# A decoder layer: first stage and self attention in one program, over shared buffers and PSUM banks, with unit 0's row maxima behind the last value copy

## What is computed

```python
q = proj(WQ_w, WQ_b)
k = proj(WK_w, WK_b)
v = proj(WV_w, WV_b)
q = _apply_rope(q, cos, sin)
k = _apply_rope(k, cos, sin)
scores = jnp.einsum('bhqd,bhkd->bhqk', q, k) / jnp.sqrt(jnp.asarray(D_K, x.dtype))
scores = jnp.where(causal[None, None, :, :], scores, -jnp.inf)
attn = jax.nn.softmax(scores, axis=-1)
out = jnp.einsum('bhqk,bhkd->bhqd', attn, v)
```

## Time and profile before

| | us |
|---|---|
| median of 3 runs | 1196.13 |
| all runs | 1196.43, 1190.45, 1196.13 |
| the profiled execution, its own time | 1199.54 |
| its span, first to last instruction | 1197.8 |
| busy in the span: PE / DVE / ACT / POOL | 1032.9 / 865.8 / 591.1 / 288.3 |
| mean granted TensorE clock (1.00 is 2.4 GHz, 0.50 is 1.2 GHz) | 0.918 |

### The profile page before, as it was taken

The page is one execution under the profiler, slowest core; times in us unless marked ns, Lnnn a source line. Parts: engine busy times, 40 slices in busy tenths (PEclk is TensorE's granted clock), DMA queues, the critical chain, the costliest instruction groups (busy, mean ns, idle before and its releaser), DMA issues. The chain is left out here.

```text
span 1197.8 us, 17928 instructions
## 1 busy us (share of the span) xinstructions
PE 1032.9 (86%) x6184; PEld 509.8 (43%) x6184; DVE 865.8 (72%) x1770; ACT 591.1 (49%) x819; POOL 288.3 (24%) x268
## 2 busy tenths in 40 slices
PE   7629999989999999989889779989889769889960
PEld 4312333333333333326778622322323218678850
DVE  5839999878898888604789968887778815645545
ACT  1311466656766667774644226645555443333322
POOL 6720101220510300012310055402020211322225
PEclk9956999999999999999999959998989888999995
DMA  5450279190200000000101034201010001242225
GB/s 192 156 145 1 36 72 106 22 154 25 56 1 1 2 1 2 1 1 31 53 27 38 1 107 144 65 25 57 23 63 28 27 26 44 68 141 73 71 83 168
DMA packets 60825, 70.04 MB, mean 58 GB/s; under 512 B 10364, under 2 KB 53756, under 8 KB 60732
## 3 DMA queue, kind: packets, MB, share of 16 engines
q1 hardware_dynamic: 55212, 57.40, 20.5%
q0 software_dynamic: 3408, 9.34, 2.2%
q10 hardware_dynamic: 2112, 2.10, 0.5%
HBM read 45.37 MB, written 22.85 MB: 57 GB/s over the span
## 5 line engine op out<-in xcount | busy, mean ns | idle before, releaser
L573 DVE TENSOR_REDUCE self_piece_max<-self_max 128x1 f32<-128x512 f32 (+3 forms) x640 | 349.6, 603 | 49.5 <-PE self_max L475 29.3
L540 ACT ACTIVATE self_probs<-self_scores 128x1024 f32<-128x1024 f32 (+3 forms) x320 | 274.3, 896 | 196.5 <-PE self_scores L494 195.5
L475 PE MATMUL self_max<-stack_k,stack_q 96*128 96x512 bf16 (+3 forms) x640 | 209.8, 366 | 6.0 <-DVE self_piece_max L573 3.9
L1732 DVE TENSOR_REDUCE cross_piece_max<-banks 128x1 f32<-128x512 f32 x256 | 164.3, 683 | 40.7 <-PE banks L1622 39.0
L1704 ACT ACTIVATE cross_probs<-banks 128x1024 f32<-128x1024 f32 x128 | 126.7, 1023 | 108.3 <-PE banks L1645 102.4
L494 PE MATMUL self_scores<-stack_q,stack_k 98*128 98x512 bf16 (+3 forms) x640 | 171.1, 351 | 7.2 <-DMA stack_q<-self_shift 5.9
L505 PE MATMUL self_out<-self_probs,V 128*17 128x512 f32 (+3 forms) x1280 | 148.4, 536 | 2.6 <-ACT self_probs L540 2.0
L475 PEld LDWEIGHTS self_max<-stack_k,stack_q 96*128 96x128 bf16 x640 | 62.3, 98 | 172.8 <-DVE self_piece_max L573 129.3
L451 POOL TENSOR_SCALAR_AFFINE_SELECT self_probs<-self_probs 128x512 f32<-128x512 f32 x64 | 40.8, 637 | 382.2 <-ACT self_probs L540 381.9
L1622 PE MATMUL banks<-kx_few,stackx 97*128 97x512 bf16 x256 | 99.9, 432 | 18.8 <-DVE cross_shift L1743 6.9
L1645 PE MATMUL banks<-stackx,kx_few 99*128 99x512 bf16 x256 | 83.0, 410 | 0.7 <-DMA stackx<-cross_shift 0.6
(11 more groups left out here) (315 smaller groups left out, 1554.9 us busy)
## 6 DMA issues: line engine op xcount, KB each, us to landing
stack_q<-qparts SPq DMA_DIRECT2D x96, 64.0 KB, 6.7
stackx<-xparts SPq DMA_DIRECT2D x96, 64.0 KB, 2.3
xin<-sent SPq DMA_DIRECT2D x39, 129.0 KB
stack_k<-kparts SPq DMA_DIRECT2D x18, 256.0 KB, 11.3
qparts<-parts SPq DMA_DIRECT2D x8, 384.0 KB, 2.6
kparts<-parts SPq DMA_DIRECT2D x8, 384.0 KB, 3.0
xparts<-xparts_sb SPq DMA_DIRECT2D x8, 384.0 KB, 2.7
o_tok<-in_w SPq DMA_DIRECT2D x4, 768.0 KB, 5.4
```

The source lines that it names most:

```text
L475: mm = nc.tensor.matmul(slot[:, 0:pc["w"]], pc["lhsT"], pc["rhs"], start=True, stop=not pc["diag"])
L540: nc.scalar.activation(probs[:, i % 3, 2 * pair:2 * pair + 2, st["off"]:C], ps[:, 2 * pair:2 * pair + 2, st["off"]:C], ACT.Exp, scale=SCAL ...
L573: nc.vector.tensor_reduce(piece_max[:, u % 2, pc["row"], pc["at"]:pc["at"] + 1], slot[:, 0:pc["w"]], AX.X, ALU.max).then_inc(side_read, 1)
L1732: nc.vector.tensor_reduce(piece_max[:, u % 2, pc["row"], pc["at"]:pc["at"] + 1], slot[:, 0:pc["w"]], AX.X, ALU.max).then_inc(side_read, 1)
```

## The change

The two blocks become one, so the barrier between them goes, and SP's waits for all stores and for chunks 0 to 2 with it. For that the two stages must live in memory together. Two large buffers, `early` and `late`, are cut into views of both stages: `probs` lies over the inputs of the projections, the later stacks over cosines, `rest`, `turned`, `crossed` and `whole`. PSUM is one tile of 8 banks: the projection products take banks 0 to 3 (later the scores), the values 4 and 5 (later `po` and one piece bank), and the pieces 6, 7 and 5. The values thus have two banks instead of four, and PE waits for the value copy of unit n - 2 instead of n - 4.

Unit 0's pieces and turn stand behind the last projection product on PE, and on DVE between the remainders of pair 6 and those of pair 7. SP sends shift 0 ahead of the stores of units 14 and 15, and loads chunk 2 of group 0 behind it instead of among the stores; chunk 3 is loaded behind shift 1. ACT waits for chunk 0's and 2's stores before it writes `acc_sb`, which now lies over `parts`.

```diff
+            early = sb(att, "early", [P, 3 * GH * C])
+            late = sb(att, "late", [P, 36 * C + 44])
...
+            xT_sb = early_part(0, KD * T).rearrange("p (k t) -> p k t", k=KD)
+            w_sb = early_part(KD * T, 3 * KD * D).rearrange("p (w k d) -> p w k d", w=3, k=KD)
+            bv_all = early_part(KD * T + 3 * KD * D, D)
+            probs = early[:].rearrange("p (n j c) -> p n j c", n=3, j=GH)
...
+            cs = late_part(0, 2 * T).rearrange("p (n t) -> p n t", n=2)
+            rest = late_part(8, 4 * C).rearrange("p (n c) -> p n c", n=4)
+            turned = late_part(12, 4 * C).rearrange("p (n h c) -> p n h c", n=2, h=2)
+            crossed = late_part(16, 4 * C).rearrange("p (n h c) -> p n h c", n=2, h=2)
+            whole = late_part(20, 4 * C).rearrange("p (n c) -> p n c", n=4)
+            parts = late_part(24, 12 * C).bitcast(BF16).rearrange("p (n r c) -> p n r c", n=SLOTS, r=3)
+            acc_sb = late_part(24, 2 * C).rearrange("p (n c) -> p n c", n=2)
+            raw = late_part(26, 2 * (MP2 // 3)).rearrange("p (n c) -> p n c", n=2)
+            last_q = late[:, 28 * C + 44:36 * C + 44].bitcast(BF16)
...
+            stack_q += [rows.rearrange("p (c h t) -> p c h t", c=NC, h=GH) for rows in (halves(16), last_q)] + stack_q
...
+            stack_k += [rows.rearrange("p (h t) -> p h t", h=GH) for rows in (halves(0), halves(8))] + stack_k
...
+            banks = psum(att, "self_banks", [P, 8, C])
+            pq = banks[:, 0:4].rearrange("p (n h) c -> p n h c", n=2)
+            pv = banks[:, 4:6]
+            ps, po = banks[:, 0:4], banks[:, 4]
+
+            def pm(n):
+                return banks[:, (6, 7, 5)[n % SB]]
...
-                pq = psum(stage, "pq", [P, 2, KD, C])
-                pv = psum(stage, "pv", [P, 4, C])
...
-                        for i in range(2):
-                            sp.wait_ge(s_parts_out[i], 8 * len(units))
-                        sp.wait_ge(consts_in, 32)
-                        for c in range(NC - 1):
-                            sp.wait_ge(s_load[c], 16 * 2 * len(PAIRS))
...
+                    def send_shift(u):
+                        sp.wait_ge(shift_ready, u + 1)
+                        for b, dst in enumerate(works[u]["shift_to"]):
+                            sp.dma_start(dst, shift[:, u % 2, b]).then_inc(shift_in[u % 2], 16)
...
+                    for n, (t, m, c) in enumerate(units):
+                        dst = (qparts, kparts)[t].rearrange("r (p m) t -> m p r t", m=KD)[m, :, :, c * C:(c + 1) * C]
+                        if n == len(units) - KD:
+                            send_shift(0)
+                            sp.wait_ge(s_parts_out[(NC - 2) % 2], 16 * TC * (NC // 2))
+                            load(NC - 2)
+                        sp.wait_ge(p3_ready, n + 1)
+                        sp.dma_start(dst, parts[:, n % SLOTS]).then_inc(s_parts_out[c % 2], 16)
+                        if 0 < c < NC - 1 and n % 4:
+                            if n % 4 == 1:
+                                sp.wait_ge(s_parts_out[(c - 1) % 2], 16 * TC * ((c + 1) // 2))
+                            for to, there in loads[c - 1][(n % 4 - 1) * 4:n % 4 * 4]:
+                                sp.dma_start(to, there).then_inc(s_load[c - 1], 16)
+
+                    for u in range(1, len(works)):
+                        send_shift(u)
+                        if u == 1:
                             for i in range(2):
...
+                                sp.wait_ge(s_parts_out[i], 8 * len(units))
+                            load(NC - 1)
+                        if u in (2, 3):
+                            load(u + 2)
...
+                    pool.wait_ge(p3_ready, len(units))
...
+                        if n >= 2:
+                            pe.wait_ge(v_read, n - 1)
+                        for k in range(KD):
+                            last = nc.tensor.matmul(pv[:, n % 2, 0:D], xT_sb[:, k, n * P:(n + 1) * P], w_sb[:, 2, k, :],
+                                                    start=(k == 0), stop=(k == KD - 1))
...
+                        if n == 2:
+                            pe.wait_ge(v_read, len(units))
+                        if n >= SB:
...
+                    pe.wait_ge(s_ones, 7)
+                    for item in before:
+                        side_item(item)
+                    for n in range(C // P):
+                        nc.tensor.matmul(po[:, n * P:(n + 1) * P], zeros[:], zeros[:], start=True, stop=True)
...
+                        if u == 0:
+                            act.wait_ge(s_parts_out[0], 8 * len(units))
...
+                    def remainders(pair):
+                        for n in (KD * pair, KD * pair + 1):
+                            dve.wait_ge(p1_ready, n + 1)
+                            if n >= 4:
+                                dve.wait_ge(p3_ready, n - 3)
+                            nc.vector.tensor_tensor(rest[:, n % 4], whole[:, n % 4], parts[:, n % SLOTS, 0], ALU.subtract).then_inc(rest_ready, 1)
...
+                        if pair:
+                            remainders(pair - 1)
...
+                    for item in before:
+                        side_item(item)
+                    remainders(len(units) // KD - 1)
+                    for third in thirds:
+                        for item in third[0] + third[1] + third[2]:
+                            side_item(item)
```

More of the change, by code:

```diff
@@ new lines, in decoder_layer @@
+            ones_rows = [stack_k[g][KS:KS + 2, :, c * C:(c + 1) * C] for g in range(NG - 1) for c in range(NC)]
+            steps, works, first_of, before, thirds, diag_before = schedule(steps, works)
+            extra_parts = [(kt_view(there), to[0][:], to[1][:]) for there, to in ((xwq, xwq_sb), (xwkv, wkv_sb))]
+            for k in range(KD):
+                for a in range(0, MP2, MP2 // 3):
+                    extra_parts.append((ctxT[k * P:(k + 1) * P, a:a + MP2 // 3].rearrange("(o p) d -> p o d", o=1),
+                                        ctx2[0][:, k:k + 1, a:a + MP2 // 3], ctx2[1][:, k:k + 1, a:a + MP2 // 3]))
```

721 lines of the change are left out of this document (318 added, 403 removed).

## The result

The changed kernel takes 1177.1 us (median of 4 runs, 1174.5 to 1180.42), the kernel before 1194.76 beside it (median of 4, 1190.45 to 1196.43). The ratio is 0.9858, with a 95% interval of 0.9833 to 0.9882: faster by 17.7 us. Forecast were 1175.8 us and 20.35 us off, and a range of 1168 to 1182. The total held. One term of the sum did not, and most of what follows is about it.

A forecast was written before the change was run, and what follows sets the result against it. The seam before self attention was taken as one serial chain ending at step 0's scores (89.50). Starting them at 69.0, less 0.15, saves 20.35 us: 1196.13 becomes 1175.8 us, range 1168 to 1182.

The forecast's parts named there:

- (1): Unit 0's reductions on DVE: start at 57.52, shift 0 ready 8.30 us later, at 65.82.
- (5): Two V banks instead of four in the projection stage: 0.15 us lost; 6 us if the cover failed in all seven pairs.
- (2): SP's queue: shift 0, behind the stores of units 12 and 13, is issued at 66.0.
- (3): Shift 0's transfer: landed and scores of step 0 started at 69.0, between bounds of 68.4 and 69.6.
- (4): Zeroing matmuls on PE, 2.05 us, between the transpose and step 0: hidden in the wait for the shift, cost nothing.
- (6): Remainders of pair 7 on DVE move from 61.56 to about 65.9, hidden in DVE's wait for step 0.
- (7): SP's queue behind shift 0: chunk 2's 12 loads take 5.5 us, landed by 76, 11 us to spare; later stores delayed harmlessly.
- A: Rival: TensorE's full clock returns earlier after the seam, 1.2 us more gain, at most 2.6 (1173 to 1174.6); chance 0.12.
- B: Rival: late transfers or V banks cause new waits, 1182 to 1189 us; chance 0.11 together with milder forms of D.
- C: Rival: half clock lasts into steps behind the seam where PE is the bound, slower than before, some 1202 us; chance 0.04.
- D: Rival: PE's pieces or shift 0 still wait for the whole first stage, 1187 us; milder forms share 0.11 with B.

The follow-up runs named there:

- four_banks: The changed kernel with four V banks instead of two, PE's first piece of unit 0 waiting for the last value copy; ratio to the kernel before 0.9833.
- merge_only: The changed kernel with both SP's order and DVE's order undone, leaving one block without a barrier and two V banks; ratio to the kernel before 0.9883.
- sp_order_before: The changed kernel with only SP's order undone: shift 0 and chunk 2's loads back behind all stores or among them; 1184.85 us, ratio 0.9922.
- after_again: The changed kernel itself, unchanged, run and profiled once more; 1177.3 us, ratio to the kernel before 0.9864.
- values_behind_pair: The changed kernel, two V banks, PE issuing both value products behind the pair's second projection product; ratio 0.9792, run again 0.9825 (1171.63 us).
- rest_behind_sums: The changed kernel with DVE waiting, ahead of a pair's remainders, until POOL's sums of the next pair are done; ratio to the kernel before 0.9878.
- before_second: The kernel before, unchanged (four V banks), profiled a second time; 1196.01 us.
- pieces_ahead: values_behind_pair with PE issuing 12 pieces of unit 1 ahead of step 0's scores instead of behind them; 1168.26 us, ratio to the kernel before 0.9782.

## Why the prediction was right, and where it was not

**(1) Shift ready 8.30 us behind the first reduction.** Right: 64.55 to 72.46 + 0.28 = 72.74, 8.19 us. The starting point, 57.52, was wrong, by (5).

**(2) and (3) Issue and landing.** In the changed kernel the stores of units 12 and 13 are long out when the shift is ready, so (2) doesn't bind, and the scores start 75.18 - 72.77 = 2.41 us behind the issue, which is the idle-queue row again. In four_banks, where the shift stands right behind these stores, the issue comes 53.63 us from t1 (forecast 66.0 - 12.90 = 53.10), and the scores 2.55 us later (forecast 3.0). The two errors of half a microsecond cancel: 56.18 against 69.0 - 12.90 = 56.10. The ordered-write rule of the Trainium skill ("DMA: Bandwidth & Descriptors", queues, rings and completion order) is not contradicted: in four_banks the store of unit 13, issued at 66.4, landed in 2.6 us, at 69.0, and the first shift row behind it took 2.3 us instead of 1.7, to 69.2. It costs little here: issued 0.5 us behind the store, the first row landed about 0.2 us behind it. Behind loads, in merge_only and sp_order_before, the scores start 3.15 and 3.36 us after the issue.

**(4), (6), (7) The hidden parts.** Right. The zeroing (71.95, 1.05 us) lies in the wait for the shift; the remainders of pair 7 (72.67, 1.27 us) too. POOL's splits follow at 74.06, and its first mask, at 82.49, comes 7.3 us behind the scores (97.45 - 89.50 = 7.95 before). Chunk 2's loads end at 80.1 on the queue, and unit 2's first reduction at 92.97 doesn't wait. The stores of units 14 and 15 leave at 80.13, not 73, as all of this stands 6 to 7 us later than forecast.

**(5) Two V banks at 0.15 us: this step failed.** The term was put at 0.15 us, on the grounds that "POOL begins pair 1 late anyway"; measured 50.71 - 45.01 = 5.7 us, from after_again and four_banks. The prediction had the right early row ("DVE [...] begins it some 0.75 us later"; it was 6.00 - 5.04 = 0.96), and then checked the steady state with rows of before, in which DVE waits for ACT each pair and so has slack. That assumed the changed kernel would reach the same steady state. It doesn't: with the late start of pair 1 POOL's third sum comes ahead of DVE's first remainder, their operations on SBUF then run beside each other in each pair, a pair takes 6.42 us instead of 5.98, and DVE never gains a lead again. Up to the start of pair 7 that adds 44.31 - 39.05 = 5.3 us, and the last remainders add 0.4. The sum "if the cover failed in all seven pairs, 7 x 0.85 = 6 us" was thus nearly the size of it, by another path: not PE's extra wait in each pair, but one late start that DVE and POOL then keep up. values_behind_pair shows that the queueing on PE sets it off here, rest_behind_sums that the overlap makes the long rows. The old steady state wasn't safe ground either: before_second has the long one with four banks. So 5.7 us is the distance between two ways in which this stage can run, not a fixed price of two banks; all four profiles of the new order without the queued product ran the short way, and nothing shows that they must.

**The sum.** Without (5) the forecast seam was 20.5 us, and four_banks shows 20.4. With (5) at 5.7 it would have been 20.5 - 5.7 = 14.8; measured 15.25. The runs gained 17.7 all the same, nearer to my 20.35 than the seam is. That the total came within 1.3 us of the forecast is therefore in part luck: the seam fell short by some 5 us, the runs gained 2 more than the seam, and before itself ran 1.4 us faster beside the changed kernel (1194.76) than the 1196.13 that I counted from. Against the mean of before's three profiles the seam gives 15.9, which leaves 1.8 us. In sp_order_before and merge_only as well the runs gain some 3 us more than the seam does by the first profile of before. Where these 2 to 3 us lie isn't settled: behind the seam, stretches whose code the change doesn't touch scatter by more than that from profile to profile (below).

**Rivals.** *A, the clock comes back earlier*: no. The half clock ends 25.0 us after the start of step 0 (75.2 to 100.2), 24.8 in after_again, 24.9 in four_banks and 23.3 in values_behind_pair, against 23.2, 23.8 and 24.7 in the three profiles of before, though the hole ahead of it was shorter. Only pieces_ahead, with its other step order, has 18.4. *B, a wait takes the barrier's place*: its half about the V banks came true with the sign for it that the prediction gave (reductions later than 58), at the price that it gave (6 us). It had 0.11 with the milder forms of D, which was too little. Its total (1182) still missed high, for the same reasons as above. *C* and *D*: neither happened, the gain of step 0 is there at 100 us (unit 2's first reduction at 79.1 from t1 instead of 95.0) and at 200 us (unit 5's row maximum at 176.4 instead of 191.3), and shift 0 left ahead of the loads.

## What to carry to other kernels

When a change takes away slack (here two of four banks), don't check the steady state with the old rows: ask which engine would lose its lead, and whether it can win it back. A loss that an old gap swallows is not free once the same change fills that gap, so price each part in the new order, and look at what is queued behind a new wait. Two moves past a common store queue were worth 4.15 us together, 2.8 with SP's alone and -4.9 with DVE's alone: test them as a pair. And look at a second profile of the old kernel before you call a way of running new: the long pairs were there already, hidden by the hole behind them.

## What the runs showed of the hardware

Two loops on DVE and POOL can lock in step. Two f32 tensor_tensor of 128x512 on DVE take 1.29 us apart from POOL's sums and 3.20 when they start with them, while the sums go from 2.49 to 2.94; once in step they stay so to the end of the stage, in seven of the thirteen profiles in which nothing keeps them apart, one of them of the old kernel. In these seven POOL's third sum started first, by as little as 0.02 us. The Trainium skill ("SBUF — State Buffer", Who interferes with whom) names the ground for it, an exclusive lock on the shared port, which DVE's operations with two SBUF inputs and GpSimd's operations that read SBUF compete for; the rows agree (3.20 us beside the sums, 1.29 apart). That it can make a 0.96 us delay into one of 5.7 I had not expected.

Stretches with the same code scatter between profiles of one kernel by half of what this change gives. From DVE's first copy of `few_count` (at 693.26 us in the first profile of before) to the end of the span, the three profiles of before took 504.5, 498.8 and 496.0 us, and the two of the changed kernel 496.1 and 496.4. Between the row maxima of units 6 and 7 alone the two profiles of the changed kernel differ by 4.3 us (50.3 and 46.0). Landmarks near the change, counted from a common event, agree better: step 0 stands at 61.35 in both.
